# Causal attention in one fused transformer layer: the mask moves from TensorE into VectorE's score copy, the row minimum is chained, and the written-out orders are new

## The chip, the cores and the metric

The kernel runs on one core of one Trainium2 chip. What counts is the device time in microseconds (us). The five engines of a core each work through a queue of their own: TensorE (PE: matmuls, and PEld: its weight loads), VectorE (DVE), ScalarE (ACT), GpSimd (POOL) and SyncE (SP, which here only starts transfers). They meet at semaphores: an instruction can raise one when it is done, and another can wait for a value of it.

## The reference

One layer with adaptive layer norm over 2048 tokens of 512 features: attention with 16 heads of 128 features, and then a feed-forward part with 4-bit weights. Cut to what matters here, for each head:

```
q, k, v = x @ W_Q.T, x @ W_K.T, x @ W_V.T            # 2048 x 128 each
scores  = q @ k.T                                     # 2048 x 2048
masked  = scores * mask - 1e10 * (1 - mask)           # mask: lower triangle
attn    = softmax(masked / sqrt(128))
z       = attn @ v
...
x = x + ga * (z_all_heads @ W_O.T)                    # then norm and feed-forward
```

All is float32, and the result must be near float32. The kernel gets this from single-pass fp32r matmuls by splitting each operand into a high part and a low part (`hi` and `lo`) and adding three products: hi·hi, hi·lo and lo·hi (`split_matmul`, L187 to L191). So nearly every product is three matmuls in a row on lines 189, 190 and 191.

## The kernel before, in words

The program has five stages, one after the other: a prologue (norm, modulation, transposed input `hT`), attention, the output projection, gate/up and down. The change touches attention and the making of the mask in the prologue.

Attention goes head by head. A head has 16 query tiles of 128 rows, i = 0 to 15. Tile i sees keys 0 to 128·(i+1)−1, in chunks of up to 512 keys: `n_chunks(i)` = i//4 + 1 chunks, 40 in a head. Only the last chunk of a tile holds the diagonal; its width is 128·(i mod 4 + 1) columns, but the tile whose own share is 128 columns computes 256 (`max(r + 1, 2) * P`, L811). The steps, by the letters of the order tables:

- **P** (PE): projections. `PQb.c`, `PKb.c`, `PVb.c` are quarter c of block b (512 tokens), three matmuls of 512 columns each; `PWb` is the four transpositions of V. Each unit ends in one PSUM bank, `ps_p`, which **U** empties: the high part by ACT, the low part by DVE.
- **S i.c** (PE, L801): scores of tile i, chunk c, into one of four PSUM banks `ps_s`. In the diagonal chunk a fourth matmul, a bf16 identity times a `causal` tile, adds the mask to 128 columns (L816).
- **C i.c** (DVE, L951): copies the chunk's scores (already scaled and negated) from PSUM to `probs` and takes their row minimum in the same instruction (L960; the trace shows it as TENSOR_SCALAR_CACHE_REDUCE and a short DVE_READ_ACCUMULATOR). With one chunk the minimum goes straight to `rmin`; with more, each chunk's goes to `cmin`, and a small TENSOR_REDUCE (L964) joins them. The scores are negated, so the minimum is the softmax's maximum.
- **E i** (ACT, L903): the exponential of the whole row, and its sum.
- **T i.u** (PE, L827): transposes 512 columns of the row in up to four 128x128 transpositions, into one of two PSUM banks `ps_t`. **H** (ACT, L892) and **L** (DVE, L971) take its high and low part to `pT`; the bank is free when L is done.
- **Z b.u** (PE): attn @ v for the pair of tiles 2b and 2b+1; **Y** (ACT) copies the result out. **R**, **N**, **G** deal with the sums; **X** (DVE) unpacks 4-bit weights for the later stages, whose decoding POOL does on the side.

No scheduler sets the order. `PE_ORDER`, `ACT_ORDER` and `DVE_ORDER` (L69 to L91) spell it out for one head, and each engine's loop runs its list 16 times. A `+` marks a step of the next head, a `-` one of the head before: heads overlap at the seam. In the first head the `-` steps are left out and the `+` steps run once ahead; in the last head it is the other way round.

Of the kernel before, what the change touches and what calls it, by code (L numbers as in the profile page):

```python
# [51 lines left out]

def chunks_before(i):

    return sum(n_chunks(j) for j in range(i))
# [15 lines left out]
    PQ1.3 T2.0 Z0.0 S3.0 PV1.0 PV1.1 PV1.2 PV1.3 T3.0 S4.0 PW1 S4.1 S5.0 S5.1 S6.0 Z1.0 PK2.0 PK2.1 T4.0 PK2.2
    PK2.3 T4.1 S6.1 T5.0 S7.0 S7.1 T5.1 PQ2.0 PQ2.1 PQ2.2 PQ2.3 Z2.0 T6.0 T6.1 Z2.1 PV2.0 PV2.1 PV2.2 PV2.3 T7.0
    T7.1 S8.0 PW2 S8.1 Z3.0 Z3.1 PK3.0 PK3.1 PK3.2 PK3.3 S8.2 S9.0 S9.1 S9.2 PQ3.0 PQ3.1 PQ3.2 PQ3.3 T8.0 T8.1
    S10.0 S10.1 PV3.0 PV3.1 PV3.2 PV3.3 T8.2 T9.0 S10.2 PW3 S11.0 S11.1 T9.1 T9.2 Z4.0 S11.2 Z4.1 T10.0 T10.1 Z4.2
# [5 lines left out]
    E0 H15.3- H0.0 UW0 UK1 G0- Y7- E1 E2 H1.0 UQ1 H2.0 Y0 E3 UV1 H3.0 UW1 E4 Y1 E5 H4.0 UK2 H4.1 H5.0 H5.1 E6 UQ2 E7  # L80
    H6.0 Y2 H6.1 UV2 H7.0 H7.1 UW2 Y3 UK3 E8 E9 UQ3 H8.0 H8.1 UV3 H8.2 H9.0 UW3 H9.1 H9.2 E10 H10.0 H10.1 Y4 E11
    H10.2 H11.0 E12 H11.1 H11.2 H12.0 H12.1 E13 Y5 H12.2 H12.3 E14 H13.0 H13.1 UQ0+ H13.2 H13.3 UK0+ H14.0 H14.1
    E15 H14.2 H14.3 Y6 H15.0 H15.1 UV0+ H15.2
# [1430 lines left out]
```

## Time and profile before

| | |
|---|---|
| time, median of 3 runs | 2215.63 us (2215.61 to 2218.49) |
| the profiled execution | 2216.7 us, its span 2214.6 us |
| PE busy | 2142.3 us, 97% |
| DVE busy | 1333.9 us, 60% |
| ACT busy | 1075.6 us, 49% |
| POOL busy | 718.9 us, 32% |
| mean granted TensorE clock | 0.987 of full speed |

Attention runs from 58 us to about 1697 us of the span. How to read it: matmuls are pipelined, and the printed duration of one holds the depth of the pipe, so the durations of neighbours overlap. What a matmul costs in a full stream is the distance from its start to the next one's start. On the engines' rows, "[0.53 <-DVE pT_lo L971]" means that the engine sat idle for 0.53 us before the instruction, and that the DVE instruction of line 971 ended the wait.

### The profile page before, as it was taken

What the parts mean: (1) busy time and instruction counts of PE and PEld (TensorE: products, weight loads), DVE (VectorE), ACT (ScalarE), POOL (GpSimd) and SP (SyncE); (2) the same over time, 40 slices, a digit from 0 to 9 for tenths busy, and PEclk for the clock granted to TensorE, in tenths of its full rate; (3) what the DMA queues carried; (4) which work ended last, traced back from release to release, by engine and by line L of the source; (5) the groups of instructions that cost most, each with busy time, mean ns of one, the idle gap of its engine ahead of it and who ended that gap; (6) DMA issues with size and microseconds to landing.
All of it is one profiled execution on the core that took longest, in us unless ns stands there. A gap on an engine that the chain in (4) does not pass through costs nothing. (4 is left out here: it accounts for less than half of the span.)

```text
span 2214.6 us, 37536 instructions
## 1 busy us (share of the span) xinstructions
PE 2142.3 (97%) x12561; PEld 1838.4 (83%) x12561; DVE 1333.9 (60%) x2998; ACT 1075.6 (49%) x2006; POOL 718.9 (32%) x545
## 2 busy tenths in 40 slices
PE   6899999999999999999999999999997899899899
PEld 3688889888888888888888888888886788788687
DVE  7364646556565646465565546464554577699865
ACT  4354545454554545454545545454544333588511
POOL 3333242525153333425250101010015444388400
PEclk9999999999999999999999999999999999999999
DMA  5111010111110110101110000000004677111121
GB/s 204 36 44 37 32 33 31 33 33 33 45 38 29 43 36 31 33 31 33 33 33 32 19 18 21 14 21 12 22 27 138 206 238 236 59 39 39 43 67 66
DMA packets 84003, 122.78 MB, mean 55 GB/s; under 512 B 9315, under 2 KB 49891, under 8 KB 83939
## 3 DMA queue, kind: packets, MB, share of 16 engines
q1 hardware_dynamic: 81635, 117.76, 16.3%
q10 hardware_dynamic: 2304, 4.20, 0.5%
q8 instruction: 36, 0.59, 0.1%
q14 instruction: 28, 0.23, 0.0%
HBM read 87.97 MB, written 33.95 MB: 55 GB/s over the span
## 5 line engine op out<-in xcount | busy, mean ns | idle before, releaser
L960 DVE TENSOR_SCALAR_CACHE_REDUCE probs<-ps_s 128x512 f32<-128x512 f32 (+3 forms) x640 | 371.2, 607 | 263.2 <-PE ps_t L827 116.4
L971 DVE TENSOR_TENSOR pT_lo<-ps_t,pT_hi 128x512 fp32r<-128x512 f32 (+3 forms) x640 | 368.9, 605 | 248.6 <-ACT pT_hi L892 247.3
L892 ACT ACTIVATE pT_hi<-ps_t 128x512 fp32r<-128x512 f32 (+3 forms) x640 | 318.6, 531 | 230.5 <-PE ps_t L827 229.6
L903 ACT ACTIVATE probs<-probs,rmin 128x128 f32<-128x128 f32 (+15 forms) x256 | 308.1, 1204 | 137.2 <-DVE rmin L964 111.9
L189 PE MATMUL ps_z<-pT_hi,v_hi 128*128 128x256 f32 (+1 forms) x1152 | 333.4, 289 | 0.0
L189 PE MATMUL ps_p<-hT_hi,w_hi 128*128 128x512 f32 x768 | 319.9, 417 | 8.7 <-PEq L269 4.1
L191 PE MATMUL ps_z<-pT_hi,v_lo 128*128 128x256 f32 (+1 forms) x1152 | 324.7, 282 | 0.0
L190 PE MATMUL ps_z<-pT_lo,v_hi 128*128 128x256 f32 (+1 forms) x1152 | 324.7, 282 | 0.0
L827 PE MATMUL ps_t<-ident,probs 128*128 128x128 f32 x2176 | 309.1, 273 | 4.5 <-DVE pT_lo L971 2.5
L191 PE MATMUL ps_p<-hT_hi,w_lo 128*128 128x512 f32 x768 | 303.1, 395 | 0.0
L190 PE MATMUL ps_p<-hT_lo,w_hi 128*128 128x512 f32 x768 | 301.1, 392 | 0.0
L827 PEld LDWEIGHTS ps_t<-ident,probs 128*128 128x128 f32 x2176 | 254.0, 140 | 39.9 <-DVE pT_lo L971 2.8
L189 PE MATMUL ps_s<-kT_hi,qT_hi 128*128 128x512 f32 (+2 forms) x640 | 262.1, 409 | 0.0
L191 PE MATMUL ps_s<-kT_hi,qT_lo 128*128 128x512 f32 (+2 forms) x640 | 233.8, 365 | 0.0
L190 PE MATMUL ps_s<-kT_lo,qT_hi 128*128 128x512 f32 (+2 forms) x640 | 233.4, 365 | 0.0
L190 PEld LDWEIGHTS ps_z<-pT_lo,v_hi 128*128 128x128 f32 x1152 | 220.2, 191 | 2.7
L189 PEld LDWEIGHTS ps_z<-pT_hi,v_hi 128*128 128x128 f32 x1152 | 220.0, 191 | 2.7
L191 PEld LDWEIGHTS ps_z<-pT_hi,v_lo 128*128 128x128 f32 x1152 | 219.7, 191 | 0.0
L233 POOL TENSOR_TENSOR w_hi<-w_raw,zeros 128x512 fp32r<-128x512 f32 x48 | 50.0, 1042 | 481.5 <-PE ps_p L191 481.5
L727 POOL TENSOR_TENSOR turn<-zeros 128x1 f32<-128x1 f32 x33 | 6.4, 193 | 552.1 <-DVE words L990 552.1
L189 PEld LDWEIGHTS ps_p<-hT_hi,w_hi 128*128 128x128 f32 x768 | 146.4, 191 | 33.2 <-issue 4.9
L191 PEld LDWEIGHTS ps_p<-hT_hi,w_lo 128*128 128x128 f32 x768 | 144.8, 189 | 33.5
(136 smaller groups left out, 3813.7 us busy)
## 6 DMA issues: line engine op xcount, KB each, us to landing
scratch_zT<-z SPq DMA_DIRECT2D x256, 64.0 KB, 1.6
o_z<-scratch_zT SPq DMA_DIRECT2D x31, 512.0 KB, 7.2
o_scales<-scratch_recips SPq DMA_DIRECT2D x31, 512.0 KB, 8.0
w_raw<-in_w_qkv SPq DMA_DIRECT2D x16, 768.0 KB, 4.5
p_wmod<-in_w_mod SPq DMA_DIRECT2D x6, 1024.0 KB, 10.6
...
```

What stands on the lines that cost most here:

```text
L189: nc.tensor.matmul(dst, stat[0], mov[0], start=start, stop=False)
L190: nc.tensor.matmul(dst, stat[0], mov[1], start=False, stop=False)
L191: return nc.tensor.matmul(dst, stat[1], mov[0], start=False, stop=stop)
L233: nc.gpsimd.tensor_tensor(st.w_hi[:, m, :], st.w_raw[:, m, :], st.zeros[:, 0:1].to_broadcast([P, DC * DH]), ALU.add) \
L727: then(nc.gpsimd.tensor_tensor(turn[:, :], zeros[:, 0:1], zeros[:, 0:1], ALU.add))
L827: last = nc.tensor.transpose(ps_t[:, n % 2, (k - 4 * u) * P:(k - 4 * u + 1) * P], probs[:, i % 2, k * P:(k + 1) * P], ident[:, :])
L892: nc.scalar.activation(pT[0][:, slot, i % 2, 0:w], ps_t[:, (chunks_before(i) + u) % 2, 0:w], ACT.Copy).then_inc(t_hi, 1)
L903: nc.scalar.activation(probs[:, i % 2, 0:w], probs[:, i % 2, 0:w], ACT.Exp, bias=rmin[:, i % 2:i % 2 + 1], scale=-1.0, accum_out=sums[:, i ...
L960: nc.vector.tensor_scalar(probs[:, i % 2, c * BT:c * BT + w], ps_s[:, at % NB, 0:w], 1.0, None, ALU.mult, ALU.min, accum_out=least).then_i ...
L971: nc.vector.tensor_tensor(pT[1][:, slot, i % 2, 0:w], ps_t[:, (chunks_before(i) + u) % 2, 0:w], pT[0][:, slot, i % 2, 0:w].bitcast(F32), A ...
```

## The change

- `causal` is now 128x512 float32 in SBUF: 384 columns of zeros, then the 128-column triangle. POOL makes it in the prologue, with one more memset.
- The bf16 mask matmul (L816) is gone, 16 of them in a head. In the diagonal chunk DVE's copy becomes `tensor_tensor_reduce`: it adds the last w columns of `causal` to the scores and takes the minimum.
- The minimum is chained: each chunk starts from the minimum of the chunk before (a scalar operand read from `cmin`), so the diagonal chunk leaves the row's minimum in `rmin`, and the TENSOR_REDUCE of tiles 4 to 15 is gone (12 in a head). For this each chunk but a tile's first waits until the one before has finished (24 in a head). A memset of one column (`lead`) stands ahead of each diagonal chunk's copy.
- The diagonal chunk of tiles 0, 4, 8 and 12 is 128 columns instead of 256.
- E waits for the count of copied chunks instead of `min_ready`.
- All three orders are new. Steps T stand together more often: the groups of adjacent transpositions on PE go from 31 in a head to 22. V's first projection is no longer a `+` step, and four more T and Z steps of the old head cross the seam.

```diff
 PE_ORDER = """
-    S0.0 T15.2- Z7.0- T15.3- T0.0 PW0 Z7.1- Z7.2- PK1.0 PK1.1 PK1.2 PK1.3 Z7.3- N0- S1.0 S2.0 PQ1.0 PQ1.1 T1.0 PQ1.2
+    S0.0 Z6.3- PV0.0 PV0.1 T14.3- T15.0- PV0.2 PV0.3 T15.1- T15.2- S1.0 Z7.0- PW0 T15.3- T0.0 Z7.1- PK1.0 PK1.1 PK1.2
...
-            n = BT if c < b else max(r + 1, 2) * P
+            n = BT if c < b else (r + 1) * P
             k = [part[:, c * BT:c * BT + n] for part in kT]
-            diagonal = c == b
-            last = split_matmul(nc, ps_s[:, at % NB, 0:n], q, k, True, True)
-            if diagonal:
-                last = nc.tensor.matmul(ps_s[:, at % NB, r * P:(r + 1) * P], ident_bf[:, :], causal[:, :],
-                                        start=False, stop=True, skip_group_check=True)
-            last.then_inc(scores_ready, 1)
+            split_matmul(nc, ps_s[:, at % S_BANKS, 0:n], q, k, True, True).then_inc(scores_ready, 1)
...
-            if n_chunks(i) == 1:
-                act.wait_ge(row_copied, CHUNKS * h + chunks_before(i) + 1)
-            else:
-                act.wait_ge(min_ready, (NT - TPB) * h + i - TPB + 1)
+            act.wait_ge(row_copied, CHUNKS * h + chunks_before(i + 1))
...
-            least = rmin[:, i % 2:i % 2 + 1] if nch == 1 else cmin[:, i % 2, c:c + 1]
-            nc.vector.tensor_scalar(probs[:, i % 2, c * BT:c * BT + w], ps_s[:, at % NB, 0:w], 1.0, None,
-                                    ALU.mult, ALU.min, accum_out=least).then_inc(row_copied, 1)
-            if nch > 1 and c == nch - 1:
-                dve.wait_ge(row_copied, CHUNKS * h + chunks_before(i) + nch)
-                nc.vector.tensor_reduce(rmin[:, i % 2:i % 2 + 1], cmin[:, i % 2, 0:nch], AX_X, ALU.min) \
-                  .then_inc(min_ready, 1)
+            least = rmin[:, i % 2:i % 2 + 1] if c == nch - 1 else cmin[:, i % 2, c:c + 1]
+            least_before = cmin[:, i % 2, c - 1:c] if c else None
+            if c:
+                dve.wait_ge(row_copied, CHUNKS * h + at)
+            out = probs[:, i % 2, c * BT:c * BT + w]
+            if c < nch - 1:
+                ins = nc.vector.tensor_scalar(out, ps_s[:, at % S_BANKS, 0:w], 1.0, least_before,
+                                              ALU.mult, ALU.min, accum_out=least)
+            else:
+                nc.vector.memset(lead[:, i % 2:i % 2 + 1], 0.0)
+                ins = nc.vector.tensor_tensor_reduce(out=out, in0=ps_s[:, at % S_BANKS, 0:w], in1=causal[:, BT - w:BT],
+                                                     scale=1.0, scalar=least_before if c else 3e38, op0=ALU.add, op1=ALU.min,
+                                                     accum_out=least)
+            ins.then_inc(row_copied, 1)
```

Three places show what moves. The first is PE's queue at the start of a middle head: S0.0, and behind it what is left of the head before (ps_t is T, ps_z is Z, ps_p is P; the rows ISA and REGISTER_ALU are waits). Before:

```order
L189 MATMUL ps_s<-kT_hi,qT_hi 128x256
L190 MATMUL ps_s<-kT_lo,qT_hi 128x256
L191 MATMUL ps_s<-kT_hi,qT_lo 128x256
L816 MATMUL ps_s<-causal,ident_bf 128x128
L825 ISA
L827 MATMUL ps_t<-ident,probs 128x128 x4
```

After, from the second half of V's projection on: T14.3 and T15.0, two quarters of PV0, T15.1 and T15.2, and then S1.0:

```order
L831 MATMUL ps_t<-ident,probs 128x128 x3
L826 ISA
L829 REGISTER_ALU
L831 MATMUL ps_t<-ident,probs 128x128 x4
L197 MATMUL ps_p<-hT_hi,w_hi 128x512
L198 MATMUL ps_p<-hT_lo,w_hi 128x512
L199 MATMUL ps_p<-hT_hi,w_lo 128x512
L197 MATMUL ps_p<-hT_hi,w_hi 128x512
L198 MATMUL ps_p<-hT_lo,w_hi 128x512
L199 MATMUL ps_p<-hT_hi,w_lo 128x512
L829 REGISTER_ALU
L831 MATMUL ps_t<-ident,probs 128x128 x4
```

T stands in pairs with only six matmuls of 512 columns between one pair and the next, and more of the old head's tail runs behind the new head's first scores.

The second is DVE's queue in the first head at tile 4, which has two chunks. Before:

```order
L960 TENSOR_SCALAR probs,cmin<-ps_s 128x512
L971 TENSOR_TENSOR pT_lo<-ps_t,pT_hi 128x512
L948 TENSOR_TENSOR v_lo<-ps_p,v_hi 128x512
L960 TENSOR_SCALAR probs,cmin<-ps_s 128x128
L964 TENSOR_REDUCE rmin<-cmin 128x1
```

After (the ISA rows are the custom instruction and its accumulator's read-out):

```order
L965 TENSOR_SCALAR probs,cmin<-ps_s 128x512
L968 MEMSET lead 128x1
L969 ISA probs,rmin<-ps_s,causal,cmin 128x128
L969 ISA rmin 128x1
```

The reduce behind the diagonal chunk became a memset ahead of it, and the diagonal copy reads `causal` and `cmin` as well.

The third is PE's queue in the first head, from the first scores on. Before, where PV0 has already run:

```order
L189 MATMUL ps_s<-kT_hi,qT_hi 128x256
L190 MATMUL ps_s<-kT_lo,qT_hi 128x256
L191 MATMUL ps_s<-kT_hi,qT_lo 128x256
L816 MATMUL ps_s<-causal,ident_bf 128x128
L827 MATMUL ps_t<-ident,probs 128x128
L787 MATMUL ps_p<-ident,vT 128x128 x4
```

After, behind S0.0 and the twelve matmuls of PV0:

```order
L197 MATMUL ps_s<-kT_hi,qT_hi 128x256
L198 MATMUL ps_s<-kT_lo,qT_hi 128x256
L199 MATMUL ps_s<-kT_hi,qT_lo 128x256
L796 MATMUL ps_p<-ident,vT 128x128 x4
L831 MATMUL ps_t<-ident,probs 128x128
```

Between the first scores and the first transposition there now stand PV0, S1.0 and PW0, where there was nothing.

## Rows read from the trace of the kernel before

**Rows 1.** Busy time by stretch of the span; attention, and its first microseconds.
```profile
58.00:1697.00 1639.00, 1629.87 (x10380) 1429.08 (x10381) 918.37 (x2419) 816.30 (x1551) 482.90 (x397) 1.00 0.10 32
70.00:81.00 11.00, 7.51 (x32) 5.87 (x32) 1.28 (x4) 3.59 (x7) 0.00 (x0) 0.84 0.00 0
```

**Rows 2.** Groups by line and shape: busy us, mean ns | idle before, releasers.
```profile
L827 PE MATMUL ps_t<-ident,probs 128*128 128x128 f32 x2176 | 309.1, 273 | 4.5 <-DVE pT_lo L971 2.5 <-ACT probs L903 2.1
```

**Rows 3.** Timeline, PE: start us, us, what; a mask matmul ahead of scores.
```profile
1007.00 0.23 PE L816 MATMUL ps_s<-causal,ident_bf 128*128 128x128 bf16 x1
1007.04 0.48 PE L189 MATMUL ps_s<-kT_hi,qT_hi 128*128 128x512 f32 x1
1007.35 0.40 PE L190 MATMUL ps_s<-kT_lo,qT_hi 128*128 128x512 f32 x1
```

**Rows 4.** Timeline, PE: a mask ahead of transpositions; transpositions in fours.
```profile
1013.07 0.23 PE L816 MATMUL ps_s<-causal,ident_bf 128*128 128x128 bf16 x1
1013.14 0.61 PE L827 MATMUL ps_t<-ident,probs 128*128 128x128 f32 x4
1013.50 0.48 PE L189 MATMUL ps_s<-kT_hi,qT_hi 128*128 128x512 f32 x1
```

**Rows 5.** Timeline, PE: eight transpositions together, and what follows.
```profile
1677.71 1.04 PE L827 MATMUL ps_t<-ident,probs 128*128 128x128 f32 x8
1678.50 0.47 PE L189 MATMUL ps_s<-kT_hi,qT_hi 128*128 128x512 f32 x1
1678.81 0.39 PE L190 MATMUL ps_s<-kT_lo,qT_hi 128*128 128x512 f32 x1
1679.04 0.40 PE L191 MATMUL ps_s<-kT_hi,qT_lo 128*128 128x512 f32 x1
```

**Rows 6.** Timeline, PE: products of 256 and of 128 columns.
```profile
1008.77 0.28 PE L191 MATMUL ps_z<-pT_hi,v_lo 128*128 128x256 f32 x1
1008.89 0.22 PE L189 MATMUL ps_z<-pT_hi,v_hi 128*128 128x128 f32 x1
...
1009.17 0.44 PE L189 MATMUL ps_p<-hT_hi,w_hi 128*128 128x512 f32 x1
1009.45 0.39 PE L190 MATMUL ps_p<-hT_lo,w_hi 128*128 128x512 f32 x1
```

**Rows 7.** Timeline, DVE: a reduce that waits, and copies that don't.
```profile
1108.82 0.08 DVE L960 DVE_READ_ACCUMULATOR probs<-ps_s 128x1 f32 x1
1108.93 0.15 DVE L964 TENSOR_REDUCE rmin<-cmin 128x1 f32<-128x2 f32 x1
1109.05 0.69 DVE L960 TENSOR_SCALAR_CACHE_REDUCE probs<-ps_s 128x512 f32<-128x512 f32 x1
1109.67 0.08 DVE L960 DVE_READ_ACCUMULATOR probs<-ps_s 128x1 f32 x1
1109.67 0.42 DVE L960 TENSOR_SCALAR_CACHE_REDUCE probs<-ps_s 128x256 f32<-128x256 f32 x1
```

**Rows 8.** Timeline, PE and DVE: transpositions, their low part, the bank reused.
```profile
1688.74 1.06 PE L827 MATMUL ps_t<-ident,probs 128*128 128x128 f32 x8 [0.53 <-DVE pT_lo L971]
...
1690.03 1.29 DVE L971 TENSOR_TENSOR pT_lo<-ps_t,pT_hi 128x512 fp32r<-128x512 f32 x2 [0.97 <-ACT pT_hi L892]
...
1690.78 0.66 PE L827 MATMUL ps_t<-ident,probs 128*128 128x128 f32 x4 [0.98 <-DVE pT_lo L971]
```

**Rows 9.** Timeline, PE: the first head's waits.
```profile
73.83 0.33 PE L827 MATMUL ps_t<-ident,probs 128*128 128x128 f32 x1 [2.07 <-ACT probs L903]
...
76.01 0.59 PE L189 MATMUL ps_p<-hT_hi,w_hi 128*128 128x512 f32 x1 [1.41 <-DVE v_lo L948]
...
82.03 0.50 PE L189 MATMUL ps_p<-hT_hi,w_hi 128*128 128x512 f32 x1 [0.35 <-DVE kT_lo L948]
```

**Rows 10.** One line's instructions, DVE: duration ns min/median/max (L971, L1187).
```profile
L971 DVE TENSOR_TENSOR pT_lo<-ps_t,pT_hi x640: 278/680/693, 74.5 to 1694.0; 128x512 fp32r<-128x512 f32 x128, 128x128 fp32r<-128x128 f32 x16, 128x384 fp32r<-128x384 f32 x16
...
L1187 DVE TENSOR_TENSOR o_x<-o_x x16: 691/2170/2584, 1731.5 to 1903.5; 128x512 f32<-128x512 f32 x16
```

More of the change, by code:

```diff
@@ L50, in n_chunks, with freed @@
     return i // TPB + 1
+def freed(h, n, banks):
+    last = n - banks if n >= banks else max(m for m in range(CHUNKS) if m % banks == n % banks) - CHUNKS
+    return CHUNKS * h + last + 1
 def chunks_before(i):
@@ L69 @@
 PE_ORDER = """
-    S0.0 T15.2- Z7.0- T15.3- T0.0 PW0 Z7.1- Z7.2- PK1.0 PK1.1 PK1.2 PK1.3 Z7.3- N0- S1.0 S2.0 PQ1.0 PQ1.1 T1.0 PQ1.2
[L71 to L74, printed above, removed]
@@ L75 @@
-    S12.0 S12.1 T10.2 S12.2 S12.3 PQ0.0+ S13.0 T11.0 S13.1 T11.1 S13.2 S13.3 T11.2 Z5.0 S14.0 T12.0 T12.1 Z5.1 Z5.2
-    T12.2 T12.3 S14.1 S14.2 S14.3 S15.0 S15.1 S15.2 T13.0 T13.1 S15.3 PQ0.1+ PQ0.2+ PQ0.3+ T13.2 Z6.0 T13.3 PK0.0+
-    PK0.1+ PK0.2+ PK0.3+ T14.0 T14.1 Z6.1 Z6.2 T14.2 T14.3 Z6.3 PV0.0+ PV0.1+ T15.0 T15.1 PV0.2+ PV0.3+
+    S0.0 Z6.3- PV0.0 PV0.1 T14.3- T15.0- PV0.2 PV0.3 T15.1- T15.2- S1.0 Z7.0- PW0 T15.3- T0.0 Z7.1- PK1.0 PK1.1 PK1.2
+    PK1.3 Z7.2- S2.0 PQ1.0 PQ1.1 PQ1.2 PQ1.3 Z7.3- N0- T1.0 T2.0 PV1.0 PV1.1 PV1.2 PV1.3 S3.0 Z0.0 PW1 S4.0 S4.1 S5.0
@@ new lines @@
+    T3.0 S5.1 S6.0 PK2.0 PK2.1 PK2.2 PK2.3 Z1.0 T4.0 T4.1 S6.1 S7.0 S7.1 T5.0 T5.1 PQ2.0 PQ2.1 PQ2.2 PQ2.3 Z2.0 Z2.1
+    T6.0 T6.1 S8.0 S8.1 S8.2 PV2.0 S9.0 T7.0 T7.1 PV2.1 S9.1 S9.2 PV2.2 PV2.3 Z3.0 PW2 T8.0 T8.1 Z3.1 PK3.0 PK3.1
+    PK3.2 PK3.3 S10.0 T8.2 T9.0 S10.1 PQ3.0 PQ3.1 PQ3.2 PQ3.3 S10.2 T9.1 T9.2 S11.0 S11.1 PV3.0 PV3.1 PV3.2 PV3.3
+    S11.2 Z4.0 PW3 T10.0 T10.1 Z4.1 Z4.2 S12.0 S12.1 T10.2 T11.0 S12.2 S12.3 S13.0 T11.1 T11.2 Z5.0 S13.1 S13.2 S13.3
+    Z5.1 Z5.2 T12.0 T12.1 S14.0 S14.1 S14.2 S14.3 T12.2 T12.3 PQ0.0+ PQ0.1+ PQ0.2+ PQ0.3+ T13.0 T13.1 S15.0 S15.1
@@ L78 @@
+    PK0.0+ T13.2 S15.2 PK0.1+ S15.3 PK0.2+ T13.3 T14.0 PK0.3+ Z6.0 Z6.1 Z6.2 T14.1 T14.2
 """
 ACT_ORDER = """
[L80 to L83, printed above, removed]
+    E0 UV0 H15.1- H15.2- UW0 H15.3- H0.0 E1 UK1 E2 UQ1 G0- Y7- H1.0 H2.0 UV1 Y0 E3 UW1 E4 H3.0 E5 UK2 Y1 H4.0 H4.1
@@ L84 @@
+    H5.0 H5.1 E6 UQ2 E7 Y2 H6.0 H6.1 H7.0 H7.1 E8 UV2 E9 UW2 H8.0 H8.1 Y3 UK3 H8.2 H9.0 UQ3 H9.1 H9.2 E10 UV3 E11 UW3
+    H10.0 H10.1 Y4 H10.2 H11.0 H11.1 H11.2 E12 E13 Y5 H12.0 H12.1 H12.2 H12.3 UQ0+ H13.0 H13.1 E14 H13.2 H13.3 H14.0
+    UK0+ E15 H14.1 H14.2 Y6 H14.3 H15.0
 """
 DVE_ORDER = """
-    C0.0 L15.2- L15.3- L0.0 UW0 UK1 C1.0 C2.0 X0 L1.0 UQ1 L2.0 C3.0 C4.0 L3.0 UW1 C4.1 C5.0 C5.1 L4.0 C6.0
-    UK2 L4.1 X1 L5.0 L5.1 C6.1 C7.0 C7.1 UQ2 L6.0 L6.1 L7.0 L7.1 C8.0 UW2 C8.1 C8.2 UK3 C9.0 C9.1 C9.2 UQ3
@@ L88 @@
-    L8.0 L8.1 C10.0 C10.1 L8.2 L9.0 UW3 C10.2 C11.0 L9.1 L9.2 X2 C11.1 C11.2 L10.0 L10.1 C12.0 C12.1 C12.2 C12.3
-    L10.2 L11.0 C13.0 L11.1 L11.2 C13.1 C13.2 L12.0 L12.1 C13.3 C14.0 C14.1 C14.2 C14.3 L12.2 L12.3 L13.0
-    L13.1 UQ0+ L13.2 C15.0 L13.3 C15.1 C15.2 C15.3 UK0+ L14.0 L14.1 R0 L14.2 L14.3 L15.0 L15.1
+    C0.0 L14.3- L15.0- L15.1- L15.2- UW0 L15.3- L0.0 C1.0 X0 UK1 C2.0 UQ1 L1.0 L2.0 C3.0 C4.0 C4.1 UW1 C5.0 C5.1 L3.0
+    UK2 C6.0 L4.0 L4.1 C6.1 X1 L5.0 L5.1 C7.0 C7.1 UQ2 C8.0 L6.0 L6.1 C8.1 C8.2 C9.0 L7.0 L7.1 C9.1 C9.2 UW2 L8.0 L8.1
@@ L91 @@
+    UK3 L8.2 C10.0 L9.0 C10.1 X2 C10.2 UQ3 L9.1 C11.0 C11.1 L9.2 C11.2 UW3 L10.0 L10.1 C12.0 L10.2 L11.0 C12.1 C12.2
+    L11.1 L11.2 C12.3 C13.0 C13.1 C13.2 C13.3 L12.0 L12.1 C14.0 L12.2 L12.3 C14.1 C14.2 C14.3 UQ0+ L13.0 L13.1 L13.2
+    C15.0 L13.3 C15.1 C15.2 C15.3 UK0+ L14.0 R0 L14.1 L14.2
 """
@@ L137 @@
 PT_SLOTS = 5
+S_BANKS = 4
+T_BANKS = 2
 def pair_chunks(b):
@@ L387, in _ @@
         nc.gpsimd.memset(start.zeros[:, :], 0.0).then_inc(start.consts, 1)
-        pool.wait_ge(start.consts, 1)
-        nc.gpsimd.affine_select(out=start.causal[:, :], in_=start.zeros[:, :], compare_op=ALU.is_ge, fill=MASKED,
+        nc.gpsimd.memset(start.causal[:, 0:BT - P], 0.0).then_inc(start.consts, 1)
+        pool.wait_ge(start.consts, 2)
+        nc.gpsimd.affine_select(out=start.causal[:, BT - P:BT], in_=start.zeros[:, :], compare_op=ALU.is_ge, fill=MASKED,
                                 base=0, pattern=[[-1, P]], channel_multiplier=1).then_inc(start.consts, 1)
```

26 lines of the change are left out of this document (13 added, 13 removed).

## The prediction

> **What bounds the kernel now.** I read the busy times by stretch first: in attention, 1639 us of the span, PE is busy for 1630 us at granted clock 1.00, DVE for 918, ACT for 816 [rows 1]. Then who waited for whom, and of that PE's part: in the whole kernel PE's transpositions, the steps that hang most on DVE and ACT, waited for 4.5 us [rows 2], all of it in the first and the last head. So in the 14 heads between, PE never waits, and the end of attention moves by what PE's stream gets shorter, as long as DVE and ACT still keep ahead. Since printed matmul durations overlap, I then read starts in the timeline, and only those give prices.
>
> **The mask matmul.** It issues 0.04 us ahead of the next matmul, which looks free, but the matmul behind it then takes 0.31 us to the next start [rows 3], where 0.23 is usual (1678.81 to 1679.04) [rows 5]: 0.04 + 0.08 = 0.12 us. Ahead of transpositions the mask takes 0.07 us [rows 4] and the next distance is as usual; I take 0.075. In a head 11 masks stand ahead of a product and 5 ahead of a transposition: 11 x 0.12 + 5 x 0.075 = 1.70 us, over 16 heads 27.1 us. All of it is on the path.
>
> **The narrow chunk.** 256 columns take 0.12 us each (1008.77 to 1008.89), three 0.36. Three of 128 take 0.28 us, and the 512-column matmul behind them 0.28 instead of 0.23 [rows 6]: 0.33 together, so 0.03 saved. A width of half the columns saves far less than half: at 128 columns something other than the columns sets the pace, 0.11 a matmul from the second on. 4 chunks x 16 heads x 0.03 = 1.9 us (bounds: 0 if what follows costs 0.08 instead of 0.05, 5.1 if it costs nothing).
>
> **Transpositions together.** Eight in a row take 0.79 us, and the next distance is 0.31 instead of 0.23: 0.87 us, 0.109 each [rows 5]. Four take 0.36 [rows 4], with the same 0.08 behind them 0.44, 0.110 each. The penalty after a group is paid back by its last member, which issues almost at once. Going from 31 to 22 groups therefore saves nothing: 9 x 16 x 0.005 is under 1 us. I take 0. The bound above is the whole 0.08 for each of 144 groups, 11.5 us.
>
> **DVE and ACT.** In a head 12 reduces go. One costs DVE 0.11 us of waiting for the accumulator and 0.12 until the next start [rows 7]: 2.8 us. The 24 chained waits cost the same 0.11 each, since without a wait the next copy starts together with the read-out [rows 7]: 2.6 us. 16 memsets of one column, nearest row the reduce at 0.12: 1.9 us (0 to 0.23 each). `tensor_tensor_reduce` isn't in the trace. It reads PSUM and one SBUF tile as L971 does, 0.68 us and at most 0.69; the upper bound is L1187 with two SBUF tiles, 2.17 us [rows 10]. I take L971's: the copies it replaces also take 0.69 [rows 7]. DVE gains about 1.7 us a head on 57 (918/16), while a head of PE becomes 100 us. It has room, so this is worth 0 unless a single step comes late. On the chain from the last score to the exponential, tiles 4 to 15 lose the reduce and its wait (0.23) and get a memset and perhaps a wait (0.12 to 0.23): no later than before. Tiles 0 to 3 get 0.12 more.
>
> A rule speaks against this. The Trainium skill (SBUF — State Buffer, practical consequences of the shared ports) says that a DVE instruction with two SBUF inputs contends with a GpSimd instruction that reads SBUF, and one with at most one doesn't; the chained copy has `causal` and, as a scalar, `cmin` in SBUF. The trace agrees on tiles: L1187 stretches to 2.17 us and L971 never does, with POOL busy 29% of attention; on a scalar operand no run here has shown anything. By the rule with the scalar counted, the sum would be that of the rival on the other side, below.
>
> **What the new order asks for.** I laid PE's new list out by the distances above and looked at each place where a step of T needs its bank back. The tightest is the seam: between T14.3 and T15.1, which share a bank, stand T15.0 (0.44) and two quarters of PV0 (6 x 0.23 = 1.39): 1.82 us. Needed: from the start of a group (the first four of the eight are one bank) to DVE's part 1.29 us, ACT's copy in between, and 0.75 until the bank is reused, 2.04 in all, or 1.6 from the end of the four [rows 8]. That leaves 0.2 us. T15.2 behind it has its own chain, H15.0 after H14.3: 0.1 us of margin. Before, the tightest T place had 1.96 us. T5.0 has 2.02 against 1.6, with C6.0 ahead of L4.0 on DVE: it may only start after T4.1, so L4.0 ends some 0.2 us before it is needed. Scores ask less: S6.0 comes 1.82 us after S4.0 and needs only one copy (0.12 + 0.62 + about 0.3). The unpacking X1 (1.5 us of DVE) stands ahead of L5.0, which Z2.0 wants 3.0 us after T5.0; it fits with 0.4. So I expect no wait in the middle heads, with margins of 0.1 to 0.4 us at four or five places.
>
> **First head.** Before, T0.0 waited 2.07 us for the first exponential, then PK1 1.41 (from 74.3) for V's low part, and PQ1 0.35; in 70 to 81 us the granted clock was 0.84 [rows 9, 1], a third of that stretch at the lower level (1.2 GHz), after those waits: 1.8 us lost. Now PV0 and S1.0 stand between S0.0 and PW0. T0.0's wait goes. PW0 waits some 0.3 us for vT, PK1 as long as before, and PQ1, with only S2.0 ahead of it, 0.6 us more than before. 2.1 - 0.3 - 0.6 = 1.2 us, and with fewer gaps I count on the clock staying up: 1.8 more, in all 3.0 (bounds: 1.2 and 3.5).
>
> **Last head.** Without the `+` steps T12.2, T12.3, T13.0 and T13.1 stand side by side, and so nearly do T14.3, T15.0, T15.1 and T15.2. Each second pair waits about 1.2 us for its banks by rows 8, and C14's four copies, which stand ahead of L13.0, add one more wait of about 1: 4.5 us against 3.1 before, of which rows 8 show 0.53 and 0.98. I take a loss of 1.5 us (0 to 4). GpSimd's splitting of the output weights takes 38 us (16 x 2.33) from PV3 on; PE's list has 38.6 us behind PV3 and 4.5 of waits, so it stays hidden, by 5 us instead of 8.
>
> **Sum.** 27.1 + 1.9 + 0 + 3.0 - 1.5 = 30.5 us. The profiled execution took 2216.7 us (span 2214.6, 2.1 around it): 2186.2. It lies 1.1 us above the median of the runs, so the median should come to 2215.6 - 30.5 = 2185.1; I give 2185. The stages behind attention keep their instructions and their waits, and only start earlier.
>
> **Rivals.**
> 1. A margin fails. The seam, T5.0, Z2.0 and S13 have 0.1 to 0.4 us; if the memset and the chained wait cost 0.25 each instead of 0.12, or the custom copy 0.1 more than L971, one or two of these places stall by 0.2 to 0.4 us in each of 15 heads: 3 to 12 us back, 2188 to 2197. For it: margins this thin are new at the seam. Against: a late T pushes everything behind it back as well, so the same time isn't lost twice. Chance 13%.
> 2. The stretched copy, which ends slower. If `tensor_tensor_reduce` takes 2.17 us at 512 columns [rows 10], each diagonal copy is 0.4 to 1.5 us longer. Five stand right ahead of something with little room: C0.0 before L14.3, C2.0 and C10.2 before UQ1 and UQ3, C6.1 before L5.0, C3.0 before T3.0 (2.8 us from its scores). Less their margins they lose 0.3 + 0.8 + 0.7 + 0.7 + 0.7 = 3.2 us a head, 51 us: 2185 + 51 = 2236. It decides from 1.9 us lost a head (30.5/16), thus from copies of about 1.6 us. Against: one tile in SBUF is L971's case. Chance 4%.
> 3. Joining pays after all: the penalty behind a group isn't paid back in the new neighbourhoods. Up to 11.5 us more: 2174 to 2180. Against it are rows 4 and 5, which agree to 1%. Chance 3%.
> 4. The clock. If longer stretches of transpositions let it drop, eight matmuls of 512 columns at half the clock in each head cost 8 x 0.23 = 1.8 us more, 29 us in all: 2214, no change. Against: attention ran at 1.00 with groups of eight, and the new order has none longer in the middle heads. Chance 2%. The Trainium skill (TensorE: Matmul & The Clock Gate, Part 4: PE-mode transpose) says that transpositions don't count as PE being busy; by that rule grouping them is what could bring this about, and rows 5, where the matmuls after eight run at full pace, don't bear it out at this length.
>
> **How the numbers follow.** The forecast, 2181 to 2189, has 78%. Range 2179 to 2196: it takes in the forecast and the first rival and leaves out rivals 2, 3 and 4, 9 in 100 and the ends of the others. A change under 0.2% (4.4 us) can't be told from none here. Faster: 78 + 13 + 3 = 94, one off for what I haven't seen, 93%. Same: rival 4 and the upper end of 1, 3%. Slower 4%.
>
> **What would show it.** PE in attention: no row of L816, 1607 to 1609 us instead of 1639, DVE and ACT waits on PE grown. Distances of 0.23 between 512-column matmuls throughout. The custom copy at 0.68 us for 512 columns, a gap of about 0.11 behind a chained read-out, the memset near 0.1. T0.0 without a wait. Wrong would be: PE rows with an idle time behind L of T15.1, T15.2 or T5.0 in every head (rival 1), custom copies well over 0.7 us (rival 2), starts after a lone group of four at more than 0.44 for the group (rival 3), granted clock under 1.00 in the middle of attention (rival 4).

## The result, and the profile after

The changed kernel takes 2185.07 us (median of four runs, 2182.17 to 2187.85), the kernel before beside it 2215.62 us (2212.49 to 2218.49). The ratio is 0.9862, with a 95% interval from 0.9841 to 0.9884: the medians differ by 30.5 us, as forecast, and the interval runs from some 26 to 35 us. The profiled execution of the changed kernel took 2187.85 us, span 2185.9.

Busy time by stretch, in the columns of [rows 1]: us, then PE, PEld, DVE, ACT and POOL with their counts, the granted clock, the DMA share and GB/s.

```profile
58.90:1668.00 1609.10, 1598.94 (x10128) 1429.94 (x10128) 927.09 (x2483) 816.88 (x1551) 483.77 (x397) 1.00 0.10 32
58.90:70.00 11.10, 8.45 (x24) 5.94 (x24) 1.19 (x2) 1.71 (x3) 0.00 (x0) 0.74 0.31 95
70.00:81.00 11.00, 8.13 (x39) 6.34 (x39) 4.02 (x15) 3.83 (x9) 2.31 (x3) 1.00 0.00 0
```

Attention, from its first matmul's start to its last one's, went from 1639.4 to 1609.1 us in the profiled executions: 30.3 us less. Their spans differ by only 28.7 us, since attention began at 58.9 us instead of 58.0 and what lies behind it took 517.9 us instead of 517.2. Those two vary from run to run: in the profiles of all thirteen kernels here attention begins at 57.7 to 59.0 us, and the stretch behind it takes 512 to 518 us. So attention, and not the whole time, is what the terms below are held against.

The stretch from 70 to 81 us now runs at clock 1.00, where [rows 1] had 0.84. Inside attention the best measure is a head's period, from the start of one head's `recips` transposition (L857, before L853) to the next head's. Two starts of the kernel before, and then two of the changed one:

```profile
284.02 0.27 PE L853 MATMUL ps_z<-ident,recips 128*16 128x128 f32 x1
385.59 0.27 PE L853 MATMUL ps_z<-ident,recips 128*16 128x128 f32 x1
...
283.97 0.27 PE L857 MATMUL ps_z<-ident,recips 128*16 128x128 f32 x1
383.57 0.27 PE L857 MATMUL ps_z<-ident,recips 128*16 128x128 f32 x1
```

Before it was 101.57 us in each of 14 heads, now it is 99.60 in each. 14 x 1.97 = 27.6 us; the first and the last head gave the rest.

Who waited for whom, among PE's rows of attention (us in all, times, the longest):

```profile
PE ps_t L831 <- DVE pT_lo L978: 3.6, 6, 1.5
...
PE ps_p L197 <- DVE qT_lo L945: 2.3, 2, 1.5
```

These, and the shorter ones that the list goes on with, are all in the first and the last head. T's waits were 4.5 us [rows 2], of which 2.1 for the first exponential and 2.5 for low parts. The first kind is gone, the second is 3.6, all in the last head.

The narrow chunk, PE's timeline in a middle head (start us, us, what):

```profile
1086.69 0.23 PE L197 MATMUL ps_s<-kT_hi,qT_hi 128*128 128x128 f32 x1
1086.75 0.27 PE L198 MATMUL ps_s<-kT_lo,qT_hi 128*128 128x128 f32 x1
1086.86 0.28 PE L199 MATMUL ps_s<-kT_hi,qT_lo 128*128 128x128 f32 x1
1086.97 0.45 PE L197 MATMUL ps_s<-kT_hi,qT_hi 128*128 128x512 f32 x1
1087.26 0.40 PE L198 MATMUL ps_s<-kT_lo,qT_hi 128*128 128x512 f32 x1
```

Three products of 128 columns take 0.28 us (1086.69 to 1086.97) and the one behind them 0.29 instead of 0.23, as [rows 6] had it. There is no mask row behind them.

The DVE side, as groups by line and shape (count | busy us, mean ns of one | idle before), and then as the timeline of a tile with four chunks:

```profile
L965 DVE TENSOR_SCALAR_CACHE_REDUCE probs<-ps_s,cmin 128x512 f32<-128x512 f32 x192 | 143.3, 747 | 13.2 <-DVE probs L965 2.6
L965 DVE TENSOR_SCALAR_CACHE_REDUCE probs<-ps_s 128x512 f32<-128x512 f32 x192 | 132.1, 688 | 146.3 <-PE ps_t L831 93.6 <-PE ps_s L199 52.7
L969 DVE CUSTOM_DVE_ANT_0 probs<-ps_s,causal,cmin 128x512 f32<-128x512 f32 x48 | 36.0, 750 | 27.7 <-issue 27.7
L968 DVE MEMSET lead<- 128x1 f32 x256 | 15.1, 59 | 42.8 <-PE ps_t L831 19.2 <-PE ps_s L199 6.2
L969 DVE CUSTOM_DVE_ANT_0 probs<-ps_s,causal 128x512 f32<-128x512 f32 x16 | 11.0, 687 | 29.4 <-issue 29.4
```

```profile
1156.84 0.74 DVE L965 TENSOR_SCALAR_CACHE_REDUCE probs<-ps_s,cmin 128x512 f32<-128x512 f32 x1
1157.50 0.08 DVE L965 DVE_READ_ACCUMULATOR probs<-ps_s,cmin 128x1 f32 x1
1157.71 0.75 DVE L965 TENSOR_SCALAR_CACHE_REDUCE probs<-ps_s,cmin 128x512 f32<-128x512 f32 x1
1158.38 0.08 DVE L965 DVE_READ_ACCUMULATOR probs<-ps_s,cmin 128x1 f32 x1
1158.60 0.06 DVE L968 MEMSET lead<- 128x1 f32 x1
1158.64 0.75 DVE L969 CUSTOM_DVE_ANT_0 probs<-ps_s,causal,cmin 128x512 f32<-128x512 f32 x1
1159.32 0.08 DVE L969 DVE_READ_ACCUMULATOR2_ANT rmin<- 128x1 f32 x1
1159.32 0.69 DVE L948 TENSOR_TENSOR kT_lo<-ps_p,kT_hi 128x512 fp32r<-128x512 f32 x1
```

The custom copy takes 687 ns, the plain copy 688. With the scalar operand from `cmin`, both kinds of copy take 60 ns more here (747, 750). A chained copy starts 0.21 us after the start of the read-out ahead of it (1157.50 to 1157.71), while an unchained instruction starts together with it (1159.32). So one chained copy comes 0.87 us after the last (1156.84 to 1157.71), where 0.62 was usual [rows 7]. Behind such a wait the memset costs 0.04 us (1158.60 to 1158.64).

### The profile page after: what moved, and what is told of

Same layout as the page of the kernel before. It is cut to its first block and busy times, and to the rows that moved or that the text cites. A ratio compares the mean times of both kernels' runs of the same rounds, so it can differ in the third digit from the quotient of the medians.

```text
span 2185.9 us, 37375 instructions
## 1 busy us (share of the span) xinstructions
PE 2111.7 (97%) x12305; PEld 1838.7 (84%) x12305; DVE 1341.7 (61%) x3062; ACT 1076.5 (49%) x2006; POOL 719.7 (33%) x546
## 5 line engine op out<-in xcount | busy, mean ns | idle before, releaser
L978 DVE TENSOR_TENSOR pT_lo<-ps_t,pT_hi 128x512 fp32r<-128x512 f32 (+3 forms) x640 | 367.4, 605 | 110.0 <-ACT pT_hi L895 109.1
L895 ACT ACTIVATE pT_hi<-ps_t 128x512 fp32r<-128x512 f32 (+3 forms) x640 | 313.1, 532 | 228.2 <-PE ps_t L831 223.4
L197 PE MATMUL ps_z<-pT_hi,v_hi 128*128 128x256 f32 (+1 forms) x1152 | 323.9, 281 | 0.0
L197 PE MATMUL ps_p<-hT_hi,w_hi 128*128 128x512 f32 x768 | 313.5, 408 | 8.1 <-PEq L277 3.5
L831 PE MATMUL ps_t<-ident,probs 128*128 128x128 f32 x2176 | 294.3, 273 | 3.8 <-DVE pT_lo L978 3.6
L831 PEld LDWEIGHTS ps_t<-ident,probs 128*128 128x128 f32 x2176 | 251.5, 140 | 29.4 <-DVE pT_lo L978 2.7
L197 PE MATMUL ps_s<-kT_hi,qT_hi 128*128 128x512 f32 (+3 forms) x640 | 248.4, 388 | 1.5 <-DVE kT_lo L948 1.5
L199 PE MATMUL ps_s<-kT_hi,qT_lo 128*128 128x512 f32 (+3 forms) x640 | 233.6, 365 | 0.0
L198 PE MATMUL ps_s<-kT_lo,qT_hi 128*128 128x512 f32 (+3 forms) x640 | 232.7, 364 | 0.0
L965 DVE TENSOR_SCALAR_CACHE_REDUCE probs<-ps_s 128x512 f32<-128x512 f32 x192 | 132.1, 688 | 146.3 <-PE ps_t L831 93.6
```

The costliest lines, as they stand in the source:

```text
L197: nc.tensor.matmul(dst, stat[0], mov[0], start=start, stop=False)
L198: nc.tensor.matmul(dst, stat[0], mov[1], start=False, stop=False)
L199: return nc.tensor.matmul(dst, stat[1], mov[0], start=False, stop=stop)
L831: last = nc.tensor.transpose(ps_t[:, n % T_BANKS, (k - 4 * u) * P:(k - 4 * u + 1) * P], probs[:, i % 2, k * P:(k + 1) * P], ident[:, :])
L895: nc.scalar.activation(pT[0][:, slot, i % 2, 0:w], ps_t[:, (chunks_before(i) + u) % T_BANKS, 0:w], ACT.Copy).then_inc(t_hi, 1)
L965: ins = nc.vector.tensor_scalar(out, ps_s[:, at % S_BANKS, 0:w], 1.0, least_before, ALU.mult, ALU.min, accum_out=least)
```

## The experiments

The steps (S, C, T and so on) have the letters of the section on the kernel before. Where a kernel was run once, its head period (steady to 0.05 us within a run unless said) carries the verdict, not its one time.

**The new code in the old orders.** The changed kernel with the three order tables of the kernel before:

```diff
-PE_ORDER, ACT_ORDER, DVE_ORDER as changed
+PE_ORDER, ACT_ORDER, DVE_ORDER of the kernel before
```

> The changed kernel with the three order tables of the kernel before; mask in the copy, chained minimum and narrow chunk stay. Theory (PE's stream alone sets the time, each matmul has its price, the orders are worth nothing): the mask and the narrow chunk are gone as before, so a middle head takes 99.8 us (99.60 with the new orders, 101.57 before), no PE wait in the middle heads, median within 4 us of the changed kernel's 2185. Rival (the old orders were laid out for a slower PE and a reduce, and only the new ones keep it fed): PE waits in every middle head, 100.5 us or more a head, median 2200 or more.

Measured: 2198.95 us (2196.43 to 2199.75), ratio 0.9922 [0.9906, 0.9939]; head 100.32 us (one of the 14 at 100.51), 0.72 more than with the new orders. The waits of T on PE, in all of the kernel:

```profile
PE ps_t L831 <- DVE pT_lo L978: 6.9, 20, 1.0
```

In a middle head PE now stalls at two places by a third of a us each, once with a releaser shown:

```profile
1156.13 0.39 PE L199 MATMUL ps_s<-kT_hi,qT_lo 128*128 128x512 f32 x1
1156.69 0.85 PE L831 MATMUL ps_t<-ident,probs 128*128 128x128 f32 x6 [0.17 <-DVE pT_lo L978]
```

DVE just before it:

```profile
1153.30 0.08 DVE L965 DVE_READ_ACCUMULATOR probs<-ps_s 128x1 f32 x1
1153.50 0.75 DVE L965 TENSOR_SCALAR_CACHE_REDUCE probs<-ps_s,cmin 128x512 f32<-128x512 f32 x1
...
1155.86 0.88 DVE L978 TENSOR_TENSOR pT_lo<-ps_t,pT_hi 128x512 fp32r<-128x512 f32 x2
```

From T's predecessor on PE to T there are 0.56 us (1156.13 to 1156.69), where 0.23 is usual. The low part that T waits for (L978 at 1155.86) stands behind the four copies of tile 14, with three gaps of 0.2 us and three scalar operands between: it starts 3.18 us after the first of them (1152.68). The new orders have that low part ahead of the later copies (C14.0 L12.2 in place of C14.3 L12.2, and likewise C12.0 L10.2). The new code does stall in the old orders, so the orders matter after all.

**The new orders on the old code.**

```diff
-PE_ORDER, ACT_ORDER, DVE_ORDER of the kernel before
+PE_ORDER, ACT_ORDER, DVE_ORDER as changed
```

> The kernel before with the three new order tables and nothing else: mask matmul, reduce and wide chunk stay. Theory (a group of transpositions pays its penalty back, so joining groups is worth nothing): 101.5 to 101.7 us a middle head, median within 4 us of 2215.6. Rival (joining saves 0.08 us for each of 9 groups): 100.85 us a head, 2204 in all.

Measured: 2214.15 us (ten runs, 2211.99 to 2217.01), ratio 0.9997 [0.9988, 1.0007]; head 101.53 instead of 101.57. Going from 31 groups of transpositions to 22 saves 0.04 us a head, next to nothing. The orders alone are worth nothing, and are needed only for something in the new code.

**Which something: the chain undone, in the new orders and in the old.** The copy's scalar operand, the waits between chunks and E's wait go back; the TENSOR_REDUCE of tiles 4 to 15 returns:

```diff
-            if c:
-                dve.wait_ge(row_copied, CHUNKS * h + at)
-                ins = nc.vector.tensor_scalar(out, ..., 1.0, least_before, ALU.mult, ALU.min, accum_out=least)
+                ins = nc.vector.tensor_scalar(out, ..., 1.0, None, ALU.mult, ALU.min, accum_out=least)
...
+            if nch > 1 and c == nch - 1:
+                dve.wait_ge(row_copied, CHUNKS * h + chunks_before(i) + nch)
+                nc.vector.tensor_reduce(rmin[:, i % 2:i % 2 + 1], cmin[:, i % 2, 0:nch], AX_X, ALU.min) \
+                  .then_inc(min_ready, 1)
```

> The changed kernel with the minimum no longer chained: tensor_tensor_reduce and the new orders stay, each chunk's minimum goes to cmin, no chained wait, and the TENSOR_REDUCE and its wait are back. Theory (VectorE has cover enough in the new orders, PE's stream alone counts): 99.60 us a middle head as with the chain, DVE's work shorter by some 4 us a head (a chained chunk starts 0.26 us later than an unchained one, 24 in a head, against 12 reduces at 0.23), median within 4 us of 2185. Rival (the chain is what makes the new orders hold, since it frees the exponential earlier): waits in the middle heads, over 99.9 us a head, 2190 or more.

> As unchained, but with the order tables of the kernel before. Theory (the 0.72 us a head that old_orders lost are the chain's price on VectorE, C12 and C14 end too late for L10.2 and L12.2): the waits go, 99.6 to 99.75 us a middle head, median 2186 to 2190. Rival (they come from a faster PE, or from the custom copy and its memset): still 100.2 to 100.4 us a head, median near 2199.

Measured: in the new orders 2182.94 us (2181.29 to 2186.53), ratio 0.9857 [0.984, 0.9875], head 99.57; in the old orders 2184.81 us (2182.09 to 2187.49), ratio 0.986 [0.9843, 0.9878], head 99.58. The old orders' two stalls are gone with the chain, which settles it: the 0.72 us were the price of the chain on DVE. Tile 14 in the old orders, unchained; from its first copy to the low part there are 2.57 us, and 3.18 with the chain:

```profile
1145.30 0.69 DVE L966 TENSOR_SCALAR_CACHE_REDUCE probs<-ps_s 128x512 f32<-128x512 f32 x1 [1.45 <-PE ps_t L832]
...
1147.87 0.88 DVE L983 TENSOR_TENSOR pT_lo<-ps_t,pT_hi 128x512 fp32r<-128x512 f32 x2
```

Neither version can be told from the changed kernel in time. DVE in the unchained kernel, new orders:

```profile
1147.37 0.08 DVE L966 DVE_READ_ACCUMULATOR probs<-ps_s 128x1 f32 x1
1147.37 0.69 DVE L966 TENSOR_SCALAR_CACHE_REDUCE probs<-ps_s 128x512 f32<-128x512 f32 x1
1147.99 0.55 DVE L970 CUSTOM_DVE_ANT_0 probs<-ps_s,causal 128x384 f32<-128x384 f32 x1
1148.46 0.08 DVE L970 DVE_READ_ACCUMULATOR2_ANT cmin<- 128x1 f32 x1
1148.58 0.16 DVE L976 TENSOR_REDUCE rmin<-cmin 128x1 f32<-128x4 f32 x1
```

Copies follow each other at 0.62 us (1147.37 to 1147.99), and one reduce of 0.16 us ends the tile. The chain replaces that reduce by up to three gaps of 0.21 and three times 0.06. A gap is paid only where the copy follows the copy before it directly: that is so for 14 of a head's 24 links in the new orders and for 16 in the old ones.

**The mask, left out.** In the kernel before, `diagonal = c == b` becomes `False`, so L816 never runs.

> The kernel before without the mask matmul (the mask is left out of the computation altogether, all else as before). Theory: 11 masks at 0.12 and 5 at 0.075 us go, 1.70 us a head, so 99.87 us a middle head and about 27 us less in all, 2188 to 2190. Rival (a mask costs only its 0.04 us of issue): 0.6 us a head, 10 us in all.

Measured: 2188.11 us; head 99.73, so the masks were worth 1.84 us. I laid the starts of this kernel's PE against those of the kernel before, step by step in ten heads. At 11 places two steps together give 0.125 us (0.04, then 0.08 on the next distance), at 5 places one gives 0.068: 1.72 us. The other 0.12 lies in steps of under 12 ns each; what it is stays open.

**The mask, twice.** A second, equal matmul behind L816:

```diff
+                nc.tensor.matmul(ps_s[:, at % NB, r * P:(r + 1) * P], ident_bf[:, :], causal[:, :],
+                                        start=False, stop=True, skip_group_check=True)
```

> The kernel before, with each mask matmul issued twice in a row (the mask counts double, so the values differ from the reference's; the masked part stays masked). The theory is the prediction's working of the mask: a price of its own of 0.04 to 0.07 us, and 0.08 us on the product behind it that is paid once for the group. So a second mask costs only 0.04 to 0.07 us, or up to 0.11 us if a 128-column matmul behind another 128-column one goes at the pace of rows 6: 16 in a head, 0.6 to 1.1 us (at 0.11: 1.8 us) more than 101.57 us a head, 102.2 to 102.7. The rival: a 128-column matmul of bf16 always costs what the first did, so the second adds as much as removing the first gave back, 1.84 us: 103.4 us a head, 2245 us in all. The theory gives 2226 to 2233 us.

Measured: 2230.11 us; head 102.42, 0.85 more, 0.053 for each second mask. Its PE:

```profile
1014.52 0.23 PE L816 MATMUL ps_s<-causal,ident_bf 128*128 128x128 bf16 x1
1014.59 0.22 PE L818 MATMUL ps_s<-causal,ident_bf 128*128 128x128 bf16 x1
1014.62 0.48 PE L189 MATMUL ps_s<-kT_hi,qT_hi 128*128 128x512 f32 x1
1014.93 0.39 PE L190 MATMUL ps_s<-kT_lo,qT_hi 128*128 128x512 f32 x1
```

The product behind takes 0.31 us to the next start, as behind one mask [rows 3]. Two masks cost 0.10 + 0.08, one 0.04 + 0.08. The rival's 1.84 is out: most of a mask's price is paid by the product behind it, once for a group.

**The narrow chunk alone, on the kernel before.**

```diff
-            n = BT if c < b else max(r + 1, 2) * P
+            n = BT if c < b else (r + 1) * P
```

> The kernel before with only the diagonal chunk of tiles 0, 4, 8 and 12 cut to 128 columns, mask matmul kept. Theory: each narrow chunk saves 0.03 us, 0.12 a head, 101.45 us a middle head; behind a mask instead of a product it may save up to 0.08, 0.3 a head. Rival (half the columns, half the time: 0.18 us each): 100.85 us a head, 11.5 us in all. In neither does PE wait in the middle heads.

Measured: 2212.79 us; head 101.28, 0.29 less, 0.07 a chunk and not 0.03. The mask stands behind each narrow chunk here and has already charged the next product its 0.08, so the three products give back their 0.08 and nothing is paid behind them.

**The narrow chunk undone, in the changed kernel**, by the reverse edit.

> The changed kernel with only one thing undone: the diagonal chunk of tiles 0, 4, 8 and 12 is 256 columns again. The theory (the prediction's 0.03 us a chunk, from distances that have no mask behind them): 4 x 0.03 = 0.12 us a head, 99.72 instead of 99.60 us, and 2187 us by the median. The rival: narrowing is worth what it gave when it was done alone on the kernel before, 0.29 us a head: 99.89, and 2190 us. If the first is right, the 0.29 held a part that belongs to the mask matmul behind the narrow chunk, and the two gains do not add up.

Measured: 2186.26 us; head 99.67 to 99.71, 0.07 to 0.11 more. Without a mask a narrow chunk is worth 0.02 to 0.03 us, 1.4 us over 16 heads. The theory holds; the two gains don't add up, since each holds the same 0.05 us of delay. With this price the head closes: 1.84 for the masks, 0.09 for the narrow chunks and 0.04 for the orders make 1.97.

**How much room DVE has.** The one-column memset made wider: 256 columns, then 768.

```diff
-    lead = sb("lead", [P, 2], F32)
+    lead = sb("lead", [P, 256], F32)
...
-                nc.vector.memset(lead[:, i % 2:i % 2 + 1], 0.0)
+                nc.vector.memset(lead[:, :], 0.0)
```

> The changed kernel with a memset of 256 columns instead of one ahead of each diagonal copy, some 0.25 us more of VectorE work, 16 times in a head (4 us a head). Theory (margins of 0.1 to 0.4 us at the seam, T5.0, Z2.0): one or two places start to stall, 99.7 to 100.3 us a middle head. Rival (the margins were reckoned too thin and VectorE has real room): 99.60 unchanged.

> The same with 768 columns, some 0.8 us more, 13 us a head; VectorE still has less work than a head lasts. Theory (thin margins at four or five places): each loses 0.3 to 0.7 us, 101.5 to 103.5 us a middle head, so the change would be no gain or a loss. Rival (real room): under 100.2.

Measured: with 256 columns (272 ns each instead of 59) 2184.84 us, head 99.59, in three of 14 heads 99.63: free. With 768 columns (698 ns each) 2219.18 us, head 102.1 at first and 101.4 at the end: the whole gain is gone.

But the load was smaller than the memset's length says. DVE with 256 columns:

```profile
1056.56 0.08 DVE L965 DVE_READ_ACCUMULATOR probs<-ps_s,cmin 128x1 f32 x1
1056.83 0.27 DVE L968 MEMSET lead<- 128x256 f32 x1 [0.19 <-DVE probs L965]
1057.02 0.63 DVE L969 CUSTOM_DVE_ANT_0 probs<-ps_s,causal,cmin 128x512 f32<-128x512 f32 x1
1057.58 0.08 DVE L969 DVE_READ_ACCUMULATOR2_ANT rmin<- 128x1 f32 x1
```

From one read-out to the next there are 1.02 us (1056.56 to 1057.58), and 0.94 with one column (1158.38 to 1159.32): 0.08 more, and not the 0.21 by which the memset is longer, since the copy behind it starts before the memset ends and is itself shorter (0.63 instead of 0.75). In all of attention DVE is busy for 944.9 us instead of 927.1, 1.1 us a head; 256 columns therefore show only that a delay of about 0.1 us a copy is free, not one of 0.2. With 768 columns DVE is busy for 7.7 us more in a head, and a copy behind a wait ends 0.61 us later. In a middle head PE then stalls at nine places by 0.1 to 0.5 us, four of them at a projection. What between 0.1 and 0.6 us would cost was not tried. Attention by stretch, in the columns of [rows 1]:

```profile
58.00:1703.00 1645.00, 1628.24 (x10127) 1424.12 (x10127) 1050.89 (x2483) 823.80 (x1551) 483.70 (x397) 1.00 0.10 32
```

DVE is busy for 1051 of 1645 us, 64%, and yet it costs PE 2 us a head: how much room an engine has shows at single steps, not in its share.

**A step moved to cover a wait.** In the first head PV1.0 waits for Q's low part; S3.0 is put ahead of it.

```diff
-... T1.0 T2.0 PV1.0 PV1.1 PV1.2 PV1.3 S3.0 Z0.0 PW1 ...
+... T1.0 T2.0 S3.0 PV1.0 PV1.1 PV1.2 PV1.3 Z0.0 PW1 ...
```

> The changed kernel with one step moved on PE: S3.0 stands ahead of the four quarters of PV1 instead of behind them. In the first head PV1.0 waits 1.1 us for the low part of Q's second block. The theory: that wait ends by DVE's copy, which does not depend on where S3.0 stands, so S3.0's three products (0.69 us) come to lie in the wait, it falls to about 0.4 us, and attention is 0.7 us shorter (1608.4 instead of 1609.1 us), with the middle heads unchanged at 99.60. The rival: the wait is passed on, to Z0.0 or PW1, which lose the cover that S3.0 gave them, and nothing is won in the first head (0 to 0.2 us). In the time of the whole kernel either is below what can be measured; the stretch from the first score to the last in the trace tells them apart.

Measured: 2184.73 us, attention 1611.2 us, and not 1608.4. In the first head the theory holds: the wait, taken from the starts, goes from 1.11 to 0.34 us. But every head has a new stall of 0.22 us (99.80 to 99.86 a head), in the middle of the run as here, with ACT's copy of V first:

```profile
1084.49 0.60 ACT L881 ACTIVATE vT<-ps_p 128x512 f32<-128x512 f32 x1 [2.68 <-PE ps_p L199]
...
1084.82 0.27 PE L199 MATMUL ps_z<-pT_hi,v_lo 128*128 128x128 f32 x1
1085.15 0.66 PE L796 MATMUL ps_p<-ident,vT 128*128 128x128 f32 x4
```

From 1084.82 to 1085.15 there are 0.33 us, where 0.11 is usual. PW1 transposes what ACT copies after PV1; that copy ends at 1085.09, and S3.0's 0.69 us had covered it. The rival was right on the place, and its price is one that I had ruled out ("the middle heads unchanged"): 0.77 won once, 0.24 lost in each of 15 heads, which is 2.9 us lost on balance. Attention is only 2.1 us longer (1611.2 against 1609.1), since its first matmuls ran at the lower clock for 6 matmuls here and for 10 in the changed kernel's profile, 0.8 us.

**Is there a better version?** The unchained kernel has the lowest median, 2182.94 against 2185.07, but the ranges overlap (2181.29 to 2186.53, and 2182.17 to 2187.85). I don't claim a gain. It says only that the chain isn't needed.

## Why the prediction came out right, point by point

The end is right (2185 forecast, 2185.07 measured), and so is the mechanism that carries it: PE's stream sets the time of the middle heads, and a mask's price shows on the product behind it. That the sum meets the measurement so closely is luck. The masks gave 2.3 us more than their term (29.4 instead of 27.1) and the first head 2.3 us less (0.7 instead of 3.0), and the rest (-0.5, +0.6, -0.3) nearly cancels too.

- **The mask matmul.** 1.70 us a head forecast; 1.72 at the steps where a mask stood, 1.84 by the period. The key reading, that the price shows on the product behind and not at the mask, is confirmed by the second mask at 0.053. Over 16 heads 27.5 to 29.4 us instead of 27.1.
- **The narrow chunk.** 1.9 us forecast, 1.4 measured. Alone on the old code it gave 0.29 us a head: had I taken that experiment for the price, the sum with the mask would have been 0.16 a head too large (1.84 + 0.29 against 1.97).
- **Transpositions together.** 0 forecast, 0.04 us a head measured, 0.6 in all; the third rival is out. The prediction's own rows give 0.88 - 0.87 = 0.01 us for each joining of two fours and not 0.005, so up to 1.4 us and not under 1.
- **DVE.** The custom copy was priced right (687 ns; 0.68 taken). The chained wait was not: I took the 0.11 us of the reduce that waits [rows 7], and it is 0.21, and the scalar operand's 0.06 was missing. Against that, only 14 of the 24 links pay the wait, and a memset costs 0.04 at the eight copies behind a wait and nothing at the others, where the copy starts ahead of it, and not 0.12. A head's DVE thus gets 14 x 0.21 + 24 x 0.06 + 8 x 0.04 = 4.7 us more and 12 x 0.23 = 2.8 less, 1.9 more in all, where I had 1.7 more. Busy time agrees: 927.1 instead of 918.4 us is 0.5 a head, and idle time behind read-outs adds 14 x 0.13 less 12 x 0.04 = 1.3. So the total is right because three wrong sizes cancel, and it isn't the total that decides: the same code stalls in the old orders, 0.72 us a head, where one low part comes 0.6 us late behind a tile's chained copies.
- **The margins.** I gave the seam 0.2 us. PE and DVE there:

```profile
1064.70 0.93 PE L831 MATMUL ps_t<-ident,probs 128*128 128x128 f32 x7
1065.75 1.23 DVE L978 TENSOR_TENSOR pT_lo<-ps_t,pT_hi 128x384 fp32r<-128x384 f32 x2
1066.86 1.03 PE L831 MATMUL ps_t<-ident,probs 128*128 128x128 f32 x8
```

  T14.3 has three transpositions and not four, so its low part starts 1.05 us after the group and not 1.29 [rows 8], and takes less time. By the 0.75 of rows 8, less the 0.13 for the missing columns, the bank is free at 1066.37; T15.1 comes at 1066.86. The margin is 0.5 us by this reckoning. The 256-column memset then showed that each diagonal copy can end about 0.1 us later without a stall anywhere. Rival 1 had half of its condition fulfilled (a chained link costs 0.27, the memset 0.04) and didn't come about in the new orders. Its mechanism is real all the same: it is what happened in the old ones, at two other places.
- **First head.** 3.0 us forecast, 0.7 measured: this is the term that was mis-sized most. PE's waits, from the timeline (the idle time printed is some 0.2 us less than what the starts give, since printed matmuls overlap: 0.39 us printed at a distance of 0.23):

```profile
74.37 0.66 PE L796 MATMUL ps_p<-ident,vT 128*128 128x128 f32 x4 [0.34 <-ACT vT L881]
...
76.44 0.50 PE L197 MATMUL ps_p<-hT_hi,w_hi 128*128 128x512 f32 x1 [1.30 <-DVE v_lo L948]
...
80.91 0.50 PE L197 MATMUL ps_p<-hT_hi,w_hi 128*128 128x512 f32 x1 [0.89 <-DVE kT_lo L948]
...
85.34 0.50 PE L197 MATMUL ps_p<-hT_hi,w_hi 128*128 128x512 f32 x1 [0.87 <-DVE qT_lo L945]
```

  T0.0's 2.07 us [rows 9] went, PW0's, PK1's and PQ1's waits came as forecast, and so did the clock: the cold stretch from 76 or 77 us on, six or seven matmuls at 0.43 us, is in all six kernels with the old orders and in none of the seven with the new. What I missed is the last row: with T1 and T2 joined, only five transpositions, some 0.6 us, stand between PQ1 and PV1, which waits for PQ1's low part: 0.87 us printed, 1.1 by the starts. Another 0.8 us is not the change's: the first matmuls of attention ran at 0.43 us (clock 0.74 from 58.9 to 70 us) for 10 matmuls in this run and 6 in the run before. That number was 5, 6 or 10 with either set of orders, so it varies by the run. Without it the term would have measured 1.5 us, still half of the forecast.
- **Last head.** -1.5 forecast, -1.8 measured: by the starts, waits of 4.9 us instead of 3.1. The largest is where I put it, behind T12.2, T12.3, T13.0 and T13.1:

```profile
1646.07 1.06 PE L831 MATMUL ps_t<-ident,probs 128*128 128x128 f32 x8 [1.49 <-DVE pT_lo L978]
```

- **Rival 2, the stretched copy.** Out: no custom copy took more than 752 ns, with POOL busy for 484 us of attention. Of the 48 copies of 512 columns with a scalar, 28 overlapped a POOL instruction, and they took 746 to 752 ns, the other 20 took 750 to 752. The Trainium skill (SBUF — State Buffer, practical consequences of the shared ports) says that a DVE instruction with two SBUF inputs contends with a GpSimd instruction that reads SBUF; in this trace a tile and a one-column scalar did not act as two. The scalar costs 0.06 us whether or not there is a tile beside it (L965 has none).
- **Rival 4, the clock.** Out: the granted clock is 1.00 in the middle of attention, and the matmuls behind eight transpositions run at full pace.

The sum again, from what was measured: 14 x 1.97 = 27.6, the same 1.97 in the first and the last head 3.9, first head 0.7, last head -1.8: 30.4, against 30.3 us of attention. The 0.7 and the -1.8 are sums of the waits and of the matmuls at the lower clock, by their starts, and are good to some 0.1 us.
